# Both gates ahead of the centered rows, turns ahead of logits, and expert rows scattered without an add, then read back

## What is computed

```python
x = x + ga * mamba(h)                                # end of the mamba stage
h = _layernorm(x) * (1 + cb) + sb                    # centre, scale, shift
xn = (h - mean(h)) * rsqrt(var(h) + eps) * ln_gamma + ln_beta
probs = softmax(xn @ router_w)
topv, topi = top_k(probs, 2); topv = topv / sum(topv)
out = sum over e of comb[:, e] * swiglu(xn, gate_up_w[e], down_w[e])
out = out + swiglu(xn, shared_gate_up_w, shared_down_w)
x = x + gb * out
```

## Time and profile before

| what | us |
|---|---|
| median of three runs | 1141.19 (1139.79 to 1141.57) |
| the profiled execution | 1141.29 |
| its span | 1140.0 |
| busy: PE, DVE, ACT, POOL | 1033.4, 970.8, 808.3, 538.9 |
| 39 scatters L2975, mean | 61.9, 1.588 |
| 39 gathers L2902, mean | 38.7, 0.992 |

### The profile page before, as it was taken

The page is one execution under the profiler, slowest core; times in us unless marked ns, Lnnn a source line. Parts: engine busy times, 40 slices in busy tenths (PEclk is TensorE's granted clock), DMA queues, the critical chain, the costliest instruction groups (busy, mean ns, idle before and its releaser), DMA issues. The chain is left out here.

```text
span 1140.0 us, 21250 instructions
## 1 busy us (share of the span) xinstructions
PE 1033.4 (91%) x7771; PEld 643.7 (56%) x7771; DVE 970.8 (85%) x1319; ACT 808.3 (71%) x1576; POOL 538.9 (47%) x485
## 2 busy tenths in 40 slices
PE   6899999999999887989999999899999984699984
PEld 4222222222222343468898984478898964398884
DVE  6899999999995776979999996989999996777774
ACT  3279898999999545978888845898888922255551
POOL 5400431010101121037989981049999972258884
PEclk9779999999999798799999999899999995699997
DMA  5210100000004520108999970128999967443335
GB/s 159 69 44 15 30 16 17 28 22 25 16 2 76 130 56 3 58 16 194 249 244 220 227 182 3 58 56 195 233 251 224 235 139 256 82 91 64 64 64 137
DMA packets 65608, 121.17 MB, mean 106 GB/s; under 512 B 15598, under 2 KB 33902, under 8 KB 65504
## 3 DMA queue, kind: packets, MB, share of 16 engines
q0 software_dynamic: 19872, 52.79, 24.9%
q1 hardware_dynamic: 43928, 64.82, 18.3%
q10 hardware_dynamic: 1704, 2.20, 0.6%
HBM read 58.02 MB, written 13.32 MB: 63 GB/s over the span
## 5 line engine op out<-in xcount | busy, mean ns | idle before, releaser
L2260 PEld LDWEIGHTS m_pair<-filter_w,delta_x_t 128*128 128x128 f32 x2560 | 294.0, 192 | 42.4 <-issue 42.4
L2260 PE MATMUL m_pair<-filter_w,delta_x_t 128*128 128x112 f32 (+3 forms) x2560 | 298.6, 276 | 9.0 <-DVE h_t L2287 3.5
L570 DVE TENSOR_REDUCE neg_max<-max_ps 128x1 f32<-128x1024 f32 x256 | 293.3, 1213 | 10.9 <-PE max_ps L559 10.8
L686 ACT ACTIVATE exp_scores<-score_k 128x512 f32<-128x512 f32 x512 | 273.9, 599 | 20.7 <-PE score_k L678 13.4
L2236 ACT ACTIVATE decay<-delta,a_log 128x1024 f32<-128x1024 f32 x128 | 145.7, 1142 | 49.3 <-DVE normed L2287 28.7
L559 PE MATMUL max_ps<-k_rows,q_rows 48*128 48x512 bf16 x512 | 166.7, 404 | 7.7 <-DVE neg_max L570 6.5
L2228 ACT ACTIVATE filter_w<-filter,b_t 128x112 f32<-128x112 f32 (+1 forms) x576 | 167.4, 374 | 0.0
L706 PE MATMUL score_k<-exp_scores,v_cols 128*32 128x256 f32 x2048 | 165.2, 396 | 0.0
L678 PE MATMUL score_k<-q_rows,k_rows 51*128 51x512 bf16 x512 | 162.8, 390 | 0.6 <-DMA q_rows<-neg_max_rows 0.6
L579 POOL CAST neg_max_parts<-neg_max 128x16 bf16<-128x16 f32 x16 | 3.1, 196 | 228.9 <-DVE neg_max L570 228.9
L559 PEld LDWEIGHTS max_ps<-k_rows,q_rows 48*128 48x128 bf16 x512 | 30.1, 95 | 120.7 <-DVE neg_max L570 92.7
(11 more groups left out here) (316 smaller groups left out, 1616.0 us busy)
## 6 DMA issues: line engine op xcount, KB each, us to landing
c_row<-c_rows SPq DMA_DIRECT2D x64, 512.0 KB, 6.2
x_inner<-normed POOLq DMA_DIRECT2D x16, 512.0 KB, 6.6
delta_x<-mod_memory POOLq DMA_DIRECT2D x15, 512.0 KB, 8.2
delta_x<-x_inner POOLq DMA_DIRECT2D x15, 512.0 KB, 8.2
x_inner<-h_t POOLq DMA_DIRECT2D x14, 512.0 KB, 6.0
mod_memory<-h_t POOLq DMA_DIRECT2D x14, 512.0 KB, 9.3
mod_memory<-normed POOLq DMA_DIRECT2D x12, 512.0 KB, 8.8
gate_up_all<-in_gate_up_w SPq DMA_DIRECT2D x8, 512.0 KB, 7.5
```

The costliest lines, as they stand in the source:

```text
L570: ve.tensor_reduce(nm[leg % 2][:, 4 * j + qt:4 * j + qt + 1], mps[:, bank:bank + 2, :].rearrange("p a q -> p (a q)"), AX_X, ALU.max, negat ...
L686: ac.activation(pt[a % 4][:, HEADS[r % 4], :], eps[:, bank, :], ACT.Exp, scale=SC).then_inc(*exped.up())
L2260: mm = pe.matmul(vps[blk][:, lo:hi], self.duT[b][:, c, blk * P:(blk + 1) * P], wf[g % 3][:, lo:hi], start=True, stop=True)
```

## The change

In `mamba` the first batch's aggregate and centering move behind both gates and the issue of the projection; the shift, the output adds and the statistics change their order accordingly. In `experts` two turns stand ahead of two logits; the four shared gate and up products of chunks 0 and 1 follow the first logits; VectorE clips all four chunks; a small Silu on ScalarE (`ac_silu_table`) has its table loaded early; the second choice's exponential comes later, `ve_weights` behind `ve_places`; the down products of chunks 0 and 1 stand ahead of the one-hots. The accumulating scatters become plain ones into one table `moe_out_rows` of 4096 rows, one for each token and choice, and a row for each empty place; nothing is set up in it. A scatter waits only for its tile, and VectorE for the scatter four tiles back. At the end both choices' rows are loaded in pieces of 512 bytes and added together, then to x, which stays on chip with the shared expert's part. The diff, cut:

```diff
@@ mamba @@
-        roots = [self.ln_root(self.X, 0, TB, added)]
+        for t in range(TB):
+            self.ve_ln_stat(self.X, t)
         tail.product()
         tail.add()
         gated = tail.gate_second()
-        for t in range(TB):
-            self.ve_center(t, 1, 3)
         gated += tail.gate_first()
         out = self.pe_out(NL - 1, 1, gated, self.s_hs.at())
-        added += [self.ve_out(self.X, c, out[c]) for c in (2, 3)]
-        roots.append(self.ln_root(self.X, TB, NT, added[2:]))
-        shifted = [self.ve_shift(self.N, t, 1, 3, roots[0]) for t in range(TB)]
-        self.norm_root, self.x_root = self.ln_root(self.N, 0, TB, shifted[-1:]), roots[1]
+        self.ve_ln_aggr(0, TB)
+        root = self.po_ln_root(0, TB)
+        for t in range(TB):
+            self.ve_center(t, 1, 3)
+        shifted = [self.ve_shift(self.N, t, 1, 3, root) for t in range(TB)]
+        added.append(self.ve_out(self.X, 2, out[2]))
+        self.norm_root = self.ln_root(self.N, 0, TB, shifted[-1:])
+        added.append(self.ve_out(self.X, 3, out[3]))
+        self.x_root = self.ln_root(self.X, TB, NT, added[2:])
+        self.ve_neg_mean(0, TB, self.norm_root)
         for t in range(TB, NT):
             self.ve_center(t, 1, 3)
@@ experts, helpers @@
-            sum_dram = [nc.dram_tensor(f"moe_sum{k}", (TOK + NTILE * P, D), ...) for k in range(2)]
+            y_dram = nc.dram_tensor("moe_out_rows", (2 * TOK + NTILE * P, D), F32, kind="Internal").ap()
-            def sp_put_zeros(): ...
+            def ac_silu_table():
+                ac.activation(spare[:], self.half[:], ACT.Silu).then_inc(*table.up())
-                ve.tensor_scalar(other[:], row[:], float(P + TOK), -float(TOK), ALU.is_ge, ALU.mult)
-                ve.scalar_tensor_tensor(out=row[:], in0=row[:], scalar=-float(P), in1=other[:], ...)
-                ve.tensor_tensor(dst[:], row[:], empty[:], ALU.add)
+                ve.scalar_tensor_tensor(out=dst[:], in0=row[:], scalar=-float(P), in1=empty[:], ...)
-            def ac_shared_up(c, half, bank): ...
-            def po_shared_clip(c, ready): ...
-            def sp_put_x(c, mark): ...
@@ experts, order @@
-            turn(0)
-            pe_logits(0, logits[0])
-            turn(1)
-            pe_logits(1, logits[0])
+            for c in (0, 1):
+                turn(c)
+            for c in (0, 1):
+                pe_logits(c, logits[0])
+            ac_silu_table()
+            for c in (0, 1):
+                pe_shared_up(c, 0, gates[c])
+                pe_shared_up(c, 1, ups[c])
...
-            ve_top(0, logits[0])
             for c in (2, 3):
                 turn(c)
+            for c in (2, 3):
                 pe_logits(c, logits[1])
+            for c in (0, 1):
+                ve_shared_clip(c, gates[c])
+                ac_shared_silu(c, gates[c].left)
+            ve_top(0, logits[0])
+            for c in (0, 1):
+                ve_shared_hidden(c, ups[c])
             ve_top(1, logits[1])
             masks = ve_masks()
+            ac_second()
+            pe_shared_up(2, 0, gates[2])
+            pe_shared_up(2, 1, ups[2])
+            pe_counts(masks, counts)
+            pe_shared_up(3, 0, gates[3])
+            pe_shared_up(3, 1, ups[3])
+            for c in (0, 1):
+                pe_shared_down(c, banks[c])
+            ve_places(counts)
             ve_weights()
             sp_weights()
...
             for c in (2, 3):
                 ve_shared_clip(c, gates[c])
-                ac_shared_silu(c, gates[c].left)
-            for c in range(NC):
+            for c in (2, 3):
                 ve_shared_hidden(c, ups[c])
@@ experts, ahead of and in the loop @@
-                wait_from(ve, y_put[j % 2].sem, 16 * ((j - NY) // 2 + 1))
+                wait_from(ve, y_put[j % NY].sem, 16 * (j // NY))
-                    po.wait_ge(y_put[j % 2].sem, 16 * (j // 2))
-                po.indirect_dma_start(sum_dram[j % 2], ..., compute_op=ALU.add)
+                po.indirect_dma_start(y_dram, ..., yo[j % NY][:], None)
-            for j in range(3):
+            ac_weights(0)
+            for c in (2, 3):
+                ac_shared_silu(c, gates[c].left)
+            for j in (1, 2):
                 ac_weights(j)
+            pe_shared_down(2, banks[2])
+            ve_add_shared(0)
             pe_tile_turn(0)
             ve_tile_turn(0)
-            pe_shared_down(2, banks[2])
-            ve_add_shared(0)
+            pe_shared_down(3, banks[3])
             ve_weights_down(0)
             pe_tile_turn(1)
             ve_tile_turn(1)
-            pe_shared_down(3, banks[3])
-            ve_add_shared(1)
-            ve_weights_down(1)
             pe_up(0)
+            ve_add_shared(1)
+            ve_weights_down(1)
             ve_add_shared(2)
-            ve_add_shared(3)
             ve_clip(0)
             ac_silu(0)
+            ve_add_shared(3)
             ve_hidden(0)
@@ the end @@
-                                 sum_dram[k][c * CH:(c + 1) * CH].rearrange("(p k) d -> p (k d)", p=P))
+                                 y_dram[lo:lo + CH].rearrange("(k p) d -> p k d", p=P))
-                ve.tensor_tensor(x, x, more, ALU.add)
+                ve.tensor_tensor(y, y, more, ALU.add).then_inc(*mixed.up())
+                ve.wait_ge(*mixed.at())
+                ve.tensor_tensor(x, x, y, ALU.add).then_inc(*mixed.up())
-            sp.wait_ge(*y_put[0].at())
-            ac.wait_ge(*y_put[1].at())
+            for k in range(NY):
+                sp.wait_ge(*y_put[k].at())
+                ac.wait_ge(*y_put[k].at())
```

More of the change, by code:

```diff
@@ L1466, in mamba @@
         added = [self.ve_out(self.X, c, tail.out[c]) for c in (0, 1)]
-        roots = [self.ln_root(self.X, 0, TB, added)]
+        for m in added:
+            ve.wait_ge(*m)
+        for t in range(TB):
+            self.ve_ln_stat(self.X, t)
         tail.product()
@@ L2832, in experts @@
             logits = [ring.take(b) for b in range(NB)]
-            gates, ups = {c: ring.take(2 + c) for c in (0, 1)}, {}
-            self.ve_neg_mean(0, TB, self.norm_root)
+            gates = {c: ring.take(i) for c, i in ((0, 2), (1, 3))}
+            ups = {c: ring.take(i) for c, i in ((0, 5), (1, 6))}
             apply_norm(range(TB), self.norm_root, range(4))
@@ L2884, in experts @@
                 ve_shared_clip(c, gates[c])
-                ac_shared_silu(c, gates[c].left)
-            for c in range(NC):
+            for c in (2, 3):
                 ve_shared_hidden(c, ups[c])
-            pe.wait_ge(*shared_gated.at())
-            banks = [ring.take(c) for c in range(NC)]
-            for c in (0, 1):
-                pe_shared_down(c, banks[c])
             pre.close()
```

92 lines of the change are left out of this document (26 added, 66 removed).

## The result

| | before | after |
|---|---|---|
| median, us | 1140.87 (1137.65 to 1143.38, 6 runs) | 1122.72 (1117.53 to 1125.03, 6 runs) |
| ratio | | 0.9839, 95% interval 0.9814 to 0.9864 |
| profiled execution; span | 1141.29; 1140.0 | 1125.03; 1123.4 |
| 39 scatters, mean ns | 1588 | 985 |
| 39 gathers, mean ns | 992 | 973 |

The change makes the kernel 1.6% faster, 18.2 us by the medians. The forecast was 1123.5 us.

A forecast was written before the change was run, and what follows sets the result against it. POOL's issue of two indirect DMAs per tile was taken to bound the loop. Terms -8.1 (to tile 3), -12.4 (loop), -1.0 (last scatter), +3.6 (end) sum to -17.9: forecast 1123.5 us, own range 1117 to 1129.5, whole range up to 1137.

The forecast's parts named there:

- part 5: Experts' loop: a plain scatter takes 1.0 us, PE becomes the bound at 2.79 a tile; -12.4, last scatter -1.0.
- covered, narrowly at worst: Experts' loop: about 7 us from a tile's output cover wake, scatter and issue (about 2) and landing (up to 4.7).
- Rival A: Experts' loop: a plain scatter costs 1.59 like any indirect write, POOL stays at 3.19 a tile; 1136.8 us; chance 0.12.
- rival C: Experts' loop: a plain scatter is dearer than the accumulating one, the kernel slower, 1152 us at 2.0; chance 0.03.
- parts 1 to 4: All work from the end of the mamba stage into the loop: tile 3 starts 8.1 us earlier.
- at most 1 us late: Head: four shared products queued on PE ahead of the turns delay the critical rows by 1 us at most.
- rival B: Ahead of the loop: half-clock shared products and ScalarE's tables lose another 4 us or so; 1127.5 to 1129; chance 0.10.
- part 2: Head, two turns then two logits: 7.0 us from second negated mean to last logits' copy, a gain of 3.0.
- part 1: End of the mamba stage: projection starts 2.7 us earlier, first negated mean 8.1, second 6.1.
- part 3: Router: weights' small operations behind the places cost +0.6, two row operations folded into one give -0.2.
- part 4: From the row list into the loop's first tiles: +0.6 us, bounds -0.5 and +2.5.
- part 6: Read back at the end: more adds +3.0, loads without head start and small store pieces +0.6; +3.6 together.

The follow-up runs named there:

- e3: The changed kernel with each scatter still adding, into rows of the one table zeroed ahead; 1136.77 us, one run.
- e4: The changed kernel with gathers five tiles ahead instead of six; 1126.26 us, one run.
- e5: The changed kernel with the up products of chunks 0 and 1 behind the last logits, VectorE's products with them behind the counts; 1117.08 us, one run.
- e12: The kernel before with only the new end of the mamba stage, no turn, logit or scatter changed; 1132.4 us, one run.
- e8: The changed kernel with two up products behind the logits, PE's waits for adds split by bank, `ve_weights` ahead of `ve_places` again; 1117.05 us, ratio 0.9795.
- e2: The changed kernel with accumulating scatters, two tables, their zeros and x, and the old read back restored; 1130.91 us, ratio 0.9915 against before.
- e9: The changed kernel with the read back in pieces of 2 KB, so wrong rows are added; 1122.09 us, one run.
- e10: The changed kernel without the first add of each pair at the end; 1121.19 us, one run.

## Why the prediction was right, step by step

From the own start, in us; "others" are the runs with the same code up to that step.

| step | forecast | after | others |
|---|---|---|---|
| projection starts | -2.7 | -2.1 | -2.1 to -2.8 |
| first negated mean | -8.1 | -7.9 | -7.9 to -8.6 |
| second negated mean | -6.1 | -5.6 | -5.6 to -6.3 |
| last logits' copy | -9.1 | -7.5 | -8.3 to -9.1 |
| row list | -8.7 | -7.9 | -8.7 to -9.6 |
| tile 3 | -8.1 | -7.3 | -8.2 to -8.6 |
| tile 3 to 38 | -12.4 | -12.5 | -12.5 |
| last turn to the read back | -1.0 | -1.5 | -1.5 |
| the end | +3.6 | +2.8 | +2.8 to +3.4 |
| sum | -17.9 | -18.6 | |

**The loop (part 5)** is shown, and it is two thirds of the gain. The unknown was the scatter's price; the forecast took the gather's, 1.0, and it is 0.985. Of the two bounds the form with the same absence of arithmetic was the near one, not the one with the same direction, and e3 proves it with the add put back alone. Rival A (1.59, 1136.8) and rival C fall. The cover of the gathers was right in sign and too small in size: "covered, narrowly at worst", with 0.3 us left by its numbers, has 2 to 3 (e4). The 4.70 from issue to turn at 1112.11 was taken for what a landing needs; it is a rare late one. The median landing is 2.8 in after and 2.9 in e4, the latest 4.0 and 4.8, and the trace of before has none for its gathers. Why single gathers land late is not settled.

**The head (parts 1 to 4)** came near the sum forecast, -7.3 in after and -8.2 to -8.6 in its like for -8.1, but by luck: two errors cancel, and a credit stands in the wrong place. From the second negated mean to the last logits the forecast had 7.0; it is 6.9 to 7.7 in the seven other runs with this order and 8.1 in after's profile. In it, "at most 1 us late" for the four shared products is mis-sized: started at about 957, they could take 4.4 us for that, and they took 5.2 to 6.4. The turns come 3.0 to 4.3 behind the negated mean where e5 has 1.56, so two of the products cost 1.5 to 2.7. And 3.8 was taken for the sixteen matmuls of two logits at half clock, and they took 1.95 at full clock, behind those same products. In after's own profile the products were late most (6.38 us, at 0.50 up to 964); that is rival B's mechanism, at less than half of its price. "A first gather after 988 proves B" was a bad mark: after's is at 988.90, but with an own start 2.0 later, and by the own start it comes at 55.7, and at 54.0 to 54.9 in its like, for 54.8 forecast. The credit: part 2 was given 3.0 us, and e12 shows 1.8 of it without part 2, since part 1 pulls the halves apart. The rest of the new head with the shared products ahead gives 0.1 to 1.3 more; the worth of part 2 comes out only in e5, with half of the products behind it.

**Parts 3 and 4** were forecast at +0.4 and +0.6. The first came out at -0.5 (19.3 from the logits' copy to the row list, against 19.8 before), the second at +0.6 from the row list to tile 3. The +0.6 for moving the weights behind the places is the term of part 3 that the runs don't show: putting them back gained nothing (e8). What else was saved there, no run takes apart. In part 4 0.5 was set aside for a slow tile 0. Six of the eight runs with the unsplit wait have it, 0.5 to 0.8, and after and e5 do not; it makes no difference, as PE waits for the adds in either case, 1.0 to 1.4 us behind a slow tile 0 and 1.75 to 1.95 behind a fast one.

**The end (part 6)** was right as a sum, +2.8 for +3.6 (the old end took 10.5 before, but 9.6 in e12 and 9.3 in e2, so that +2.8 to +4.6 can be read from the traces), and wrong as an account; that the sum held was luck. I took +3.0 for four more adds and nothing for the loads' small pieces, on the strength of 380 GB/s in one microsecond at launch, where other loads ran beside; the adds were to follow in an unbroken row. They do not: from the first add's start to the last one's end it is 6.9 in after against 2.8 before, +4.1, of which 1.3 are more waits for the loads. The first add comes 4.1 behind SyncE's issue instead of 5.5 (4.5 and 4.3 in e2 and e12), where the lost head start was to cost time, and that is what brings the sum down again; why it comes earlier stays open. The single removals give 1.4 to 2.1 for the pieces (e9) and 0.4 to 1.1 for the adds (e10), which cover each other. The Trainium skill, "DMA: Bandwidth & Descriptors", section "Why small descriptors are slow (HBM only)", had the direction right, where the launch row showed nothing; but an estimate by its 3 cycles for each packet makes 512 bytes 13% dearer, and the measured 290 against 403 GB/s is 39%. The measurement decides.

## What to carry to other kernels

When two instruction forms bound an unknown one, ask which shares the costly property with it, and price it by that one: here the costly property was the add, not the direction. On an engine that issues two DMAs a turn, 0.6 us more on one of them can set the whole loop's pace; look for the engine that has no idle time but its issue gaps, not for the one with the highest busy share. A wait seen in one trace is not what its removal brings: compare it over all traces with the same code (1.95 in after, 1.0 to 1.4 in six others). When a reordering moves a step earlier, run that move alone before crediting the second reordering behind it.

## What the hardware showed that was not expected

- **Pieces.** Eight loads of 256 KB from device memory moved at 290 GB/s in pieces of 512 bytes and at 403 in pieces of 2 KB, in the same place of the kernel. The median time to landing was 5.5 and 6.2 us on the two queues against 4.7 and 5.2.
- **The price of issuing.** On POOL a gather of 128 rows takes 0.97 to 1.00 in the mean of a run, a plain scatter 0.985 to 0.988, one with an add 1.59 to 1.60, and at least 0.30 lies between them.
- **The clock at the projection.** The same 32 matmuls took 3.81 in after, with the granted clock at 1.00, and 5.43 in e5, where the window from 936 to 937 shows 0.56, though PE had been idle for 2.25 us ahead of them in after and for only 1.88 in e5. It made no difference to the time, as VectorE did not wait for the projection in either. What decides it stays open.
- **The spread.** The same code up to the end of the mamba stage took between 926 and 933 us. It is larger than most edits tried here, so a single time can't judge them, and a trace read from a step that nothing changed can.
